# An adaptive feed-forward layer with a router in float32: the last four groups' first layer in two pairs by Strassen's algorithm

## The chip, the cores and the metric

The kernel runs on one core of one Trainium2 chip. Its time is the device time of one execution in microseconds, the median over several runs. Engines: PE is TensorE (matmuls), PEld its weight loads, DVE is VectorE, ACT is ScalarE, POOL is GpSimd, SP is the queue that issues most DMAs.

## What is computed

The reference, cut to its core (64 batches of N = 64 rows of D = 512; E = 6 experts of rank R = 16, the best 2 of them by router; biases and reshapes kept where they matter):

```
q_emb = relu(cond @ W3 + b3)                       # (64, 512)
x1 = (64 * x + sum(x, axis=1)) * q_emb[:, None, :] # (64, 64, 512)
y  = relu(x1 @ W2 + b2)                            # first layer, 512 x 512
gates = softmax(y @ W_router + b_router)           # 6 experts
w = gates where among the two largest, else 0
out = x + (y @ W_base + b_base) + (y @ A_s) @ B_s \
        + sum over e of w_e * ((y @ A_r[e]) @ B_r[e])
```

## The kernel before

The 4096 rows are cut into 8 groups of 512 (TG). In a group everything is transposed: features stand on the 128 partitions, in 4 chunks (KC, index c or k), rows along the free dimension. float32 accuracy comes from splitting each operand into two rounded parts, hi = round(a) and lo = a - hi (the *rest*), both of type float32r, and from three matmuls for each product: hi.hi, hi.lo, lo.hi (helper `product`, line 750).

Per group, by engine:

- **VectorE** makes the next group's x1 chunk by chunk: `turn_x` (line 474) transposes, `sum_x` (479) sums over the rows of a batch, `add_sum` (486) adds 64 x and the sum. It also makes the rests of x1 and of y (`x1_rest` 494, `y_rest` 500), the ranking of experts and the gates (`rank_experts` 547 to 570, `gates` 576 to 594), the weighted hidden layer (`weigh` 601, `hw_rest` 614) and the last addition of x (`add_x` 628).
- **GpSimd** multiplies by q_emb (`scale`, 308) and, at the start, makes the rests of the weights (`W_rest`, 314).
- **ScalarE** rounds: `x1_split` (347), `relu` (353 and 355, two instructions for each of the 4 output blocks m), `hw_split` (415); it copies the router's logits out of PSUM (`h_head`, 445, four instructions) and takes exponentials (454).
- **TensorE** runs 48 matmuls of the first layer (`m1`, four output blocks m of 12), 12 of `h` (router, shared and routed down projections in one), 48 of `m2` (y @ W_base, by 4 row tiles t), 12 of `up` (the up projections, onto the same PSUM banks as `m2`): 120 of 512 columns. `up` of group g-1 stands between the third and fourth block of m1 of group g.
- **SP** loads x twice (transposed quarters for VectorE, and as it is for the last addition), spreads the gates over the 16 ranks by four DMAs from `wT` to `gatesT`, and stores the output.

Each engine works through its own list in the order in which it is written; the engines meet in semaphores only. In the last group the gates are spread by one matmul (`expand`, 877) and hw is done in two halves. The 8 banks of PSUM are four of m2, three of m1 (the fourth block of m1 shares a bank with m2) and one, hT, for h.

## Time and profile before

| what | value |
|---|---|
| median of three runs | 235.28 us (235.24 to 235.88) |
| the profiled execution | 236.26 us, its span 234.1 us |
| TensorE busy | 229.5 us (98% of the span), 1007 matmuls |
| VectorE, ScalarE, GpSimd busy | 165.8, 86.4, 48.9 us |
| mean granted clock of TensorE | 1.000 |

The span runs from the first instruction to the last. The rows below are from this one execution; times in them are microseconds from the span's start, unless marked ns. "x3" behind a row is the number of instructions merged in it, and a bracket tells how long the engine had been idle before, and for whom. Matmuls overlap, so the 389 ns of one are not the step from one to the next.

### The profile page before, as it was taken

To read this page: it belongs to the slowest core of one execution; us is meant where nothing else is said; L and a number is where in the kernel's file an instruction comes from. 1 tells how busy PE (TensorE), PEld (TensorE's weight loads), DVE (VectorE), ACT (ScalarE), POOL (GpSimd) and SP (SyncE) were. 2 spreads that over 40 slices of the span, in tenths; PEclk is the share of its full clock that TensorE was granted. 3 is DMA by queue.
4 is the path that set the end of the run, shared out by engine and by line. 5 is a ranking of instruction groups with operands and counts; after the bars stand their busy time and mean duration, and the time that the engine had idled before them with its cause. 6 is when DMAs were issued, how large, how long until landed. Compare 5 with 4: busy or idle time off the path is not lost.

```text
span 234.1 us, 3090 instructions
## 1 busy us (share of the span) xinstructions
PE 229.5 (98%) x1007; PEld 188.3 (80%) x1007; DVE 165.8 (71%) x309; ACT 86.4 (37%) x171; POOL 48.9 (21%) x57
## 2 busy tenths in 40 slices
PE   7999999999999999999999999999999999999994
PEld 3977888888888888888888888888888888888883
DVE  0685979899889966596939969399656966064344
ACT  3178632646036330535116240263306351252430
POOL 6089334032212211013012211022111030000000
PEclk9999999999999999999999999999999999999999
DMA  6999903509270723626053641709020360104004
GB/s 207 313 229 229 276 5 79 137 3 315 67 187 4 250 111 69 144 107 255 10 134 69 194 167 26 185 4 345 12 34 0 141 218 14 21 0 179 3 0 179
DMA packets 32505, 28.80 MB, mean 123 GB/s; under 512 B 5817, under 2 KB 22909, under 8 KB 32494
## 3 DMA queue, kind: packets, MB, share of 16 engines
q1 hardware_dynamic: 30682, 28.50, 43.1%
q10 hardware_dynamic: 1812, 0.17, 0.6%
q8 instruction: 6, 0.10, 0.2%
q14 instruction: 5, 0.04, 0.0%
HBM read 18.89 MB, written 8.39 MB: 117 GB/s over the span
## 4 chain that ended last, share of the span: by engine, by line
PE 97%; DVE 1%; ACT 1%; issue 0%; DVEq 0%
PE m_ps L750 78%; PE hT L750 9%; PE m_ps L777 5%; PE m_ps L727 2%; DVE out_nat L628 1%; PE m_ps L740 1%; PE m_ps L769 1%; PE hT L740 0%; ACT qT L367 0%; ACT W_hi L373 0%; ACT x_hi L378 0%; PE m_ps L734 0%; DVE idle L468 0%; PE hT L877 0%; PE m_ps L733 0%
## 5 line engine op out<-in xcount | busy, mean ns | idle before, releaser
L308 POOL TENSOR_TENSOR x_full<-x_sum,qT 128x512 f32<-128x512 f32 x28 | 32.2, 1150 | 134.6 <-DVE x_sum L486 134.6
L353 ACT ACTIVATE y_hi<-m_ps,condT 128x512 fp32r<-128x512 f32 x32 | 22.0, 687 | 77.5 <-PE m_ps L750 77.2
L750 PE MATMUL m_ps<-Wb_lo,y_hi 128*128 128x512 f32 x128 | 49.8, 389 | 0.0
L750 PE MATMUL m_ps<-Wb_hi,y_lo 128*128 128x512 f32 x128 | 49.8, 389 | 0.0
L750 PE MATMUL m_ps<-Wb_hi,y_hi 128*128 128x512 f32 x128 | 49.8, 389 | 0.0
L750 PE MATMUL m_ps<-x_hi,W_hi 128*128 128x512 f32 x112 | 43.6, 389 | 0.0
L750 PE MATMUL m_ps<-x_hi,W_lo 128*128 128x512 f32 x112 | 43.6, 389 | 0.0
L500 DVE TENSOR_TENSOR y_lo<-m_ps,y_hi 128x512 fp32r<-128x512 f32 x32 | 21.6, 674 | 30.4 <-ACT m_ps L355 30.4
L750 PE MATMUL m_ps<-x_lo,W_hi 128*128 128x512 f32 x112 | 41.8, 389 | 0.0
L474 DVE STREAM_TRANSPOSE xT<-x_quart 128x512 f32<-128x512 f32 x28 | 30.3, 1083 | 0.0
L750 PEld LDWEIGHTS m_ps<-Wb_hi,y_hi 128*128 128x128 f32 x128 | 24.0, 188 | 5.0
L750 PEld LDWEIGHTS m_ps<-Wb_hi,y_lo 128*128 128x128 f32 x128 | 24.0, 188 | 5.0
L750 PEld LDWEIGHTS m_ps<-Wb_lo,y_hi 128*128 128x128 f32 x128 | 24.0, 188 | 5.0
L347 ACT ACTIVATE x_hi<-x_full 128x512 fp32r<-128x512 f32 x28 | 17.6, 629 | 19.1 <-POOL x_full L308 19.0
L750 PEld LDWEIGHTS m_ps<-x_hi,W_hi 128*128 128x128 f32 x112 | 21.0, 188 | 4.4
L750 PEld LDWEIGHTS m_ps<-x_hi,W_lo 128*128 128x128 f32 x112 | 21.0, 188 | 4.4
L750 PEld LDWEIGHTS m_ps<-x_lo,W_hi 128*128 128x128 f32 x112 | 21.0, 188 | 4.3
L628 DVE TENSOR_TENSOR out_nat<-m_ps,x_nat 128x512 f32<-128x512 f32 x32 | 20.5, 680 | 2.1 <-PE m_ps L750 2.1
L355 ACT ACTIVATE m_ps<-m_ps,condT 128x512 f32<-128x512 f32 x32 | 21.0, 655 | 0.0
L486 DVE SCALAR_TENSOR_TENSOR x_sum<-xT,vsum 128x512 f32<-128x512 f32 x28 | 19.4, 693 | 2.1
L494 DVE TENSOR_TENSOR x_lo<-x_full,x_hi 128x512 fp32r<-128x512 f32 x28 | 19.1, 706 | 1.6 <-ACT x_hi L347 1.6
L479 DVE TENSOR_REDUCE vsum<-xT 128x8 f32<-128x512 f32 x28 | 19.0, 679 | 0.3
(99 smaller groups left out, 256.5 us busy)
## 6 DMA issues: line engine op xcount, KB each, us to landing
out_dram<-out_nat SPq DMA_DIRECT2D x32, 256.0 KB, 2.2
x_quart<-in_x_dram SPq DMA_DIRECT2D x28, 256.0 KB, 4.5
x_nat<-in_x_dram SPq DMA_DIRECT2D x7, 1024.0 KB, 6.1
gatesT<-wT SPq DMA_DIRECT2D x28, 48.0 KB
x_nat<-in_x_dram SPq DMA_DIRECT2D x4, 256.0 KB, 3.7
W_f<-in_L_cond_W_dram SPq DMA_DIRECT2D x4, 256.0 KB, 6.7
Wb_f<-in_L_ffn_W_base_dram SPq DMA_DIRECT2D x1, 1024.0 KB, 9.2
W_sb<-in_L_cond_W_dram SPq DMA_DIRECT2D x2, 256.0 KB, 5.0
```

What stands on the lines that cost most here:

```text
L308: nc.gpsimd.tensor_tensor(per_batch(x1_full[:, c, :]), per_batch(x1_sum[:, c, :]), qT[:, c, bass.ds(BG * g, BG)].unsqueeze(2).to_broadcast ...
L347: nc.scalar.activation(x1_hi[par][:, c, :], x1_full[:, c, :], ACT.Copy).then_inc(x1_hi_ready, 1)
L353: nc.scalar.activation(y_hi[:, m, :], m1_ps[m][:, :], ACT.Relu, bias=b2_sb[:, m:m + 1]).then_inc(y_hi_ready, 1)
L355: nc.scalar.activation(m1_ps[m][:, :], m1_ps[m][:, :], ACT.Relu, bias=b2_sb[:, m:m + 1]).then_inc(y_full_ready, 1)
L474: nc.vector.transpose(xT[c % 2][:, :], x_quart[par][:, :, :].rearrange("p b (i c) -> p c b i", c=KC)[:, c]).then_inc(xT_ready, 1)
L479: nc.vector.tensor_reduce(vsum[c % 2][:, :], per_batch(xT[c % 2][:, :]), AX.X, ALU.add).then_inc(vsum_ready, 1)
L486: nc.vector.scalar_tensor_tensor(out=per_batch(x1_sum[:, c, :]), in0=per_batch(xT[c % 2][:, :]), scalar=float(N), in1=vsum[c % 2][:, :].un ...
L494: nc.vector.tensor_tensor(x1_lo[par][:, c, :], x1_full[:, c, :], x1_hi[par][:, c, :].bitcast(F32), ALU.subtract).then_inc(x1_lo_ready, 1)
L500: nc.vector.tensor_tensor(y_lo[:, m, :], m1_ps[m][:, :], y_hi[:, m, :].bitcast(F32), ALU.subtract).then_inc(y_lo_ready, 1)
L628: nc.vector.tensor_tensor(out_nat[par][:, t, :], m2_ps[t][:, :], x_nat[par][:, t, :], ALU.add).then_inc(out_ready, 1)
L750: mm = nc.tensor.matmul(psum, lhsT, rhs, start=start and i == 0, stop=stop and i == len(terms) - 1)
L777: return nc.tensor.matmul(m1_ps[m][:, :], W[:, k, m * P:(m + 1) * P], x1[0][:, k, :], start=k == 0 and W is W2_hi and x1 is x1_hi, stop=k ...
```

## The change

Groups 4 to 7 are done as pairs p = 0 (groups 4, 5) and p = 1 (groups 6, 7). The first layer of a pair is a product of 2 x 2 blocks: W2 cut into halves of output features m and of input features k, x1 into halves of k and the two groups. It is done by Winograd's form of Strassen's algorithm with seven block products instead of eight. With x11, x21 the two halves of k of the first group and x12, x22 those of the second:

- operands: T1 = x12 - x11, T2 = x22 - T1, T3 = x22 - x12, T4 = x21 - T2, each in two chunks kk = 0, 1; and weights V1 to V4, combined once from W2's quarters;
- products 1 to 7 (`PRODUCTS`), each of 6 matmuls for each half-block mh of m; TensorE runs them in `PRODUCT_ORDER`;
- results: C11, C12, C21, C22 by seven additions for each mh (`ADD_ORDER`), in VectorE, in place in PSUM, with ScalarE's copy of product 1 (`copy_p1`).

GpSimd combines the operands and makes all their rests (`prepare`), and the rests of group 3's x1 too. ScalarE rounds the 14 operands (`operand`). The chunks of a pair come in the order of `CHUNKS` as (group of the pair, c). Tiles are shared to make room: x1 is worked on in place (`xs`), hw in place in hT, the output in place in `x_nat`, so that loads of x wait for stores. The four loops over groups are written out. The `expand` matmul and the work in halves of the last group go; its gates are spread by DMA into `gates_last`.

The core of the diff (blank lines left out). The orders:

```diff
+        CHUNKS = ((0, 0), (1, 0), (1, 2), (0, 2), (0, 1), (0, 3), (1, 1), (1, 3))
+        OPERANDS = (("x11", 0), ("T1", 0), ("x22", 0), ("T2", 0), ("T3", 0), ("x21", 0), ("T4", 0),
+                    ("x11", 1), ("x21", 1), ("T1", 1), ("T2", 1), ("T3", 1), ("x22", 1), ("T4", 1))
+        COMBOS = (("T1", 0), ("T2", 0), ("T3", 0), ("T4", 0), ("T1", 1), ("T2", 1), ("T3", 1), ("T4", 1))
+        SLOTS = {("x11", 0): 8, ("T1", 0): 9, ("T2", 0): 10, ("x22", 0): 11, ("T3", 0): 12, ("x21", 0): 13, ("T4", 0): 0,
+                 ("x11", 1): 1, ("x21", 1): 2, ("T1", 1): 3, ("T2", 1): 4, ("T3", 1): 5, ("x22", 1): 6, ("T4", 1): 7}
+        PRODUCTS = {1: ("W", 0, 0, "x11", 0), 2: ("W", 2, 0, "x21", 1), 3: ("V", 2, 0, "x22", 2), 4: ("W", 2, 256, "T4", 3),
+                    5: ("V", 2, 256, "T1", 3), 6: ("V", 0, 0, "T2", 2), 7: ("V", 0, 256, "T3", 0)}
+        PRODUCT_ORDER = ((1, 2, 6, 7, 3, 5, 4), (1, 2, 6, 5, 7, 4, 3))
+        USED_BY = {operand: n for n, (_, _, _, operand, _) in PRODUCTS.items()}
+        ADD_ORDER = (("C11", "u2", "u4", "u3", "C22", "C12", "C21"), ("C11", "u2", "u4", "u3", "C22", "C21", "C12"))
+        C_BANK = {"C11": 1, "C22": 0, "C12": 2, "C21": 3}
+        Y_ORDER = ((0, 0), (1, 2), (1, 0), (0, 2), (0, 1), (1, 3), (0, 3), (1, 1))
```

GpSimd, one pair (`rest` waits for `operand` of ScalarE; `scale_pair` for VectorE's chunk):

```diff
+                scale_pair(0, 0)
+                rest("x11", 0)
+                scale_pair(1, 0)
+                T1(0)
+                scale_pair(1, 2)
+                rest("T1", 0)
+                rest("x22", 0)
+                T2(0)
+                T3(0)
+                rest("T2", 0)
+                scale_pair(0, 2)
+                rest("T3", 0)
+                rest("x21", 0)
+                T4(0)
+                scale_pair(0, 1)
+                rest("T4", 0)
+                rest("x11", 1)
+                scale_pair(0, 3)
+                scale_pair(1, 1)
+                rest("x21", 1)
+                T1(1)
+                scale_pair(1, 3)
+                rest("T1", 1)
+                T2(1)
+                T3(1)
+                rest("T2", 1)
+                rest("T3", 1)
+                rest("x22", 1)
+                T4(1)
+                rest("T4", 1)
+            for p in range(PAIRS):
+                prepare(p)
```

ScalarE, from group 3 on:

```diff
+            def operand(p, name, kk):
+                if name[0] == "T":
+                    act.wait_ge(combo_ready, nth_combo(p, name, kk))
+                else:
+                    act.wait_ge(pair_full_ready, nth_chunk(p, {"x11": 0, "x21": 0, "x22": 1}[name], kk + (0 if name == "x11" else 2)))
+                if p > 0:
+                    act.wait_ge(product_done, nth_product(p - 1, 1, USED_BY[name]))
...
+                x1_split(3, m - 1)
+            head(2)
+            exponentials(2)
+            x1_split(3, 3)
+            operand(0, "x11", 0)
+            relu(3, 0)
+            operand(0, "T1", 0)
+            hw_split(2)
+            relu(3, 1)
+            operand(0, "x22", 0)
+            operand(0, "T2", 0)
+            relu(3, 2)
+            operand(0, "T3", 0)
+            operand(0, "x21", 0)
+            relu(3, 3)
+            operand(0, "T4", 0)
+            operand(0, "x11", 1)
+            head(3)
+            exponentials(3)
+            operand(0, "x21", 1)
+            operand(0, "T1", 1)
+            def pair(p):
...
+                copy_p1(0)
+                operand(p, "T2", 1)
+                hw_split(g - 1)
+                operand(p, "T3", 1)
+                operand(p, "x22", 1)
+                relu_pair(0, 0)
+                operand(p, "T4", 1)
+                relu_pair(1, 2)
+                copy_p1(1)
+                relu_pair(1, 0)
+                relu_pair(0, 2)
+                operand_next("x11", 0)
+                relu_pair(0, 1)
+                relu_pair(1, 3)
+                relu_pair(0, 3)
+                relu_pair(1, 1)
+                operand_next("T1", 0)
+                head(g)
+                operand_next("x22", 0)
+                operand_next("T2", 0)
+                exponentials(g)
+                head(g + 1)
+                operand_next("T3", 0)
+                operand_next("x21", 0)
+                exponentials(g + 1)
+                operand_next("T4", 0)
+                operand_next("x11", 1)
+                hw_split(g)
+                operand_next("x21", 1)
+                operand_next("T1", 1)
+            for p in range(PAIRS):
+                pair(p)
+            hw_split(NG - 1)
```

VectorE, from the end of group 2 on (`whole_pair` is turn, sum and add of one chunk; `..._next` the same for the next pair):

```diff
+            rank_experts(2)
+            gates(2)
+            whole_pair(0, 0)
+            whole_pair(0, 1)
+            whole_pair(0, 2)
+            y_rest_single(3, 0)
+            weigh(2)
+            turn_pair(0, 3)
+            hw_rest(2)
+            y_rest_single(3, 1)
+            total_pair(0, 3)
+            add_x(2, 0)
+            y_rest_single(3, 2)
+            add_x(2, 1, 2, 3)
+            whole_pair(0, 4)
+            y_rest_single(3, 3)
+            whole_pair(0, 5)
+            rank_experts(3)
+            gates(3)
+            whole_pair(0, 6)
+            whole_pair(0, 7)
...
+                weigh(g - 1)
+                C11(0)
+                u_2(0)
+                hw_rest(g - 1)
+                turn_next(0)
+                y_rest_pair(0, 0)
+                sum_next(0)
+                add_x(g - 1, 0, 1)
+                u_4(0)
+                u_3(0)
+                C22(0)
+                C12(0)
+                C21(0)
+                add_x(g - 1, 2, 3)
+                y_rest_pair(1, 2)
+                C11(1)
+                y_rest_pair(1, 0)
+                u_2(1)
+                add_next(0)
+                u_4(1)
+                y_rest_pair(0, 2)
+                u_3(1)
+                C22(1)
+                C21(1)
+                y_rest_pair(0, 1)
+                C12(1)
+                y_rest_pair(1, 3)
+                y_rest_pair(0, 3)
+                y_rest_pair(1, 1)
+                turn_next(1)
+                total_next(1)
+                turn_next(2)
+                total_next(2)
                 rank_experts(g)
+                turn_next(3)
+                gates(g)
+                total_next(3)
+                rank_experts(g + 1)
+                turn_next(4)
+                gates(g + 1)
+                total_next(4)
+                weigh(g)
+                turn_next(5)
+                hw_rest(g)
+                total_next(5)
+                turn_next(6)
+                total_next(6)
+                if not more:
+                    weigh(g + 1)
+                add_x(g, 0, 1, 2, 3)
+                turn_next(7)
+                total_next(7)
+            for p in range(PAIRS):
+                pair(p)
```

TensorE, one pair:

```diff
+                    which, k0, col, operand, b = PRODUCTS[n]
+                    W_hi, W_lo = (W2_hi, W2_lo) if which == "W" else (V_hi, V_lo)
+                    cols = slice(col + mh * P, col + (mh + 1) * P)
+                    ps = m1_pair[p][mh][b][:, :]
+                    for kk in range(2):
+                        begins = kk == 0
+                        if mh == 0:
+                            pe.wait_ge(pair_hi_ready, nth_operand(p, operand, kk))
+                        product(ps, [(W_hi[:, k0 + kk, cols], hi_of(operand, kk)),
+                                     (W_lo[:, k0 + kk, cols], hi_of(operand, kk))], begins, False)
+                        if mh == 0:
+                            pe.wait_ge(pair_lo_ready, nth_operand(p, operand, kk))
+                        mm = product(ps, [(W_hi[:, k0 + kk, cols], lo_of(operand, kk))], False, kk == 1)
+                    mm.then_inc(product_done, 1)
+                if p > 0:
+                    pe.wait_ge(out_ready, TT * (g - 2) + TT)
+                blocks(0, 1)
+                blocks(0, 2)
+                if p == 0:
+                    pe.wait_ge(V_lo_ready, KC)
+                blocks(0, 6)
+                pe.wait_ge(p1_copied, 2 * p + 1)
+                blocks(0, 7)
+                pe.wait_ge(adds_ready, nth_add(p, 0, "u2"))
+                blocks(0, 3)
+                up(g - 1, 0, 1)
+                blocks(0, 5)
+                up(g - 1, 2, 3)
+                pe.wait_ge(adds_ready, nth_add(p, 0, "u4"))
+                blocks(0, 4)
+                pe.wait_ge(out_ready, TT * (g - 1) + 1)
+                blocks(1, 1)
+                pe.wait_ge(out_ready, TT * (g - 1) + 2)
+                blocks(1, 2)
+                pe.wait_ge(out_ready, TT * (g - 1) + 3)
+                blocks(1, 6)
+                pe.wait_ge(out_ready, TT * (g - 1) + 4)
+                blocks(1, 5)
+                pe.wait_ge(p1_copied, 2 * p + 2)
+                blocks(1, 7)
+                pe.wait_ge(adds_ready, nth_add(p, 1, "u4"))
+                blocks(1, 4)
+                blocks(1, 3)
+                h(g, 0)
+                h(g, 2)
+                m2(g, 0, 0, 2)
+                h(g, 1)
+                m2(g, 0, 1)
+                h(g, 3)
+                m2(g, 0, 3)
+                for k in range(KC):
+                    h(g + 1, k)
+                for t in range(1, TT):
+                    m2(g, t, *range(KC))
+                m2(g + 1, 0, *range(KC))
+                m2(g + 1, 1, *range(KC))
+                up(g, 0, 1, 2, 3)
+                m2(g + 1, 2, *range(KC))
+                pe.wait_ge(out_ready, TT * g + 1)
+                m2(g + 1, 3, *range(KC))
+                if last:
+                    up(g + 1, 0, 1, 2, 3)
```

## Rows read from the trace of the kernel before

**Rows 1.** The page: busy time by engine, and the chain's shares by engine.

```profile
PE 229.5 (98%) x1007; PEld 188.3 (80%) x1007; DVE 165.8 (71%) x309; ACT 86.4 (37%) x171; POOL 48.9 (21%) x57
...
PE 97%; DVE 1%; ACT 1%; issue 0%; DVEq 0%
```

**Rows 2.** The chain that ended last: start us, length us, what.

```profile
1.27 3.59 PE m_ps L727 x8
...
12.47 11.47 PE m_ps L777 x48
...
82.44 23.12 PE m_ps L750 x102
...
109.64 23.12 PE m_ps L750 x102
...
225.92 0.23 PE hT L877
```

**Rows 3.** Timeline of VectorE: start us, length us, line, operation, count.

```profile
60.36 1.07 DVE L474 STREAM_TRANSPOSE xT<-x_quart 128x512 f32<-128x512 f32 x1
...
62.80 0.68 DVE L494 TENSOR_TENSOR x_lo<-x_full,x_hi 128x512 fp32r<-128x512 f32 x1
...
87.00 1.25 DVE L494 TENSOR_TENSOR x_lo<-x_full,x_hi 128x512 fp32r<-128x512 f32 x2
...
90.71 1.09 DVE L474 STREAM_TRANSPOSE xT<-x_quart 128x512 f32<-128x512 f32 x1
...
95.99 0.69 DVE L500 TENSOR_TENSOR y_lo<-m_ps,y_hi 128x512 fp32r<-128x512 f32 x1 [4.19 <-ACT m_ps L355]
...
102.05 1.87 DVE L628 TENSOR_TENSOR out_nat<-m_ps,x_nat 128x512 f32<-128x512 f32 x3
...
111.22 0.31 DVE L547 STREAM_TRANSPOSE h_nat<-h_head 128x128 f32<-128x128 f32 x1 [1.79 <-ACT h_head L445]
...
113.24 0.17 DVE L576 TENSOR_REDUCE den<-expo 128x4 f32<-128x24 f32 x1
...
114.20 1.25 DVE L494 TENSOR_TENSOR x_lo<-x_full,x_hi 128x512 fp32r<-128x512 f32 x2
```

**Rows 4.** Who waited for whom: us in total, times, longest us.

```profile
POOL x_full L308 <- DVE x_sum L486: 134.6, 28, 7.6
```

**Rows 5.** Timeline of GpSimd: two rests, and one scale.

```profile
13.75 2.54 POOL L314 TENSOR_TENSOR W_lo<-W_f,W_hi 128x512 fp32r<-128x512 f32 x2 [0.67 <-ACT W_hi L373]
...
36.30 1.04 POOL L308 TENSOR_TENSOR x_full<-x_sum,qT 128x512 f32<-128x512 f32 x1 [4.85 <-DVE x_sum L486]
```

**Rows 6.** Timeline of ScalarE in group 3.

```profile
98.48 0.65 ACT L355 ACTIVATE m_ps<-m_ps,condT 128x512 f32<-128x512 f32 x1
99.05 0.63 ACT L347 ACTIVATE x_hi<-x_full 128x512 fp32r<-128x512 f32 x1
100.16 0.69 ACT L353 ACTIVATE y_hi<-m_ps,condT 128x512 fp32r<-128x512 f32 x1 [0.48 <-PE m_ps L750]
...
109.68 1.50 ACT L445 ACTIVATE h_head<-hT,h_bias 32x128 f32<-32x128 f32 x4 [1.58 <-PE hT L750]
```

**Rows 7.** Timelines of VectorE and GpSimd where the two meet.

```profile
30.84 0.66 DVE L551 TENSOR_TENSOR logit<-h_nat,lmax 128x24 f32<-128x24 f32 x1
...
30.16 1.29 POOL L314 TENSOR_TENSOR Wu_lo<-Wu_f,Wu_hi 128x512 fp32r<-128x512 f32 x1
...
125.87 0.69 DVE L614 TENSOR_TENSOR hw_lo<-hw_full,hw_hi 128x512 fp32r<-128x512 f32 x1
...
126.21 1.25 POOL L308 TENSOR_TENSOR x_full<-x_sum,qT 128x512 f32<-128x512 f32 x1 [6.90 <-DVE x_sum L486]
```

**Rows 8.** The instructions of line 551: shortest, median, longest ns.

```profile
L551 DVE TENSOR_TENSOR logit<-h_nat,lmax x8: 182/182/657, 30.8 to 220.6; 128x24 f32<-128x24 f32 x8
```

**Rows 9.** Timeline of SP's queue: issues.

```profile
114.31 3.75 SPq L263 DMA_DIRECT2D gatesT<-wT  x4
```

**Rows 10.** Windows: busy us of each engine, then the granted clock.

```profile
91.90:119.10 27.20, 27.20 (x122) 22.53 (x121) 20.46 (x38) 9.38 (x18) 4.58 (x5) 1.00 0.43 124
```

More of the change, by code:

```diff
@@ L265, in _ @@
-            step(0, 0, first=True)
-            with sp.Fori(0, (NG - 4) // 2) as pair:
-                for half in range(2):
-                    step(pair * 2 + (1 + half), (1 + half) % 2)
-            for g in range(NG - 3, NG):
-                step(g, g % 2)
-            store(NG - 1, (NG - 1) % 2, (1, 2, 3, 4))
+                    sp.wait_ge(out_ready, TT * g + 1 + max(order.index(i) for i in range(t + 1)))
+                    sp.dma_start(out_groups[g][:, t, :], x_nat[g % 2][:, t, :]).then_inc(stored[g % 2], 16)
@@ new lines, in _ @@
+            for m in range(KC):
+                relu(0, m)
+            act.wait_ge(Wu_loaded, 48)
+            nc.scalar.activation(Wu_hi[:, :], Wu_f[:, :], ACT.Copy).then_inc(Wu_hi_ready, 1)
+            x1_split(1, 0)
+            head(0)
+            x1_split(1, 1)
+            exponentials(0)
+            x1_split(1, 2)
+            x1_split(1, 3)
+            hw_split(0)
+            for m in range(KC):
+                relu(1, m)
+                if m >= 2:
+                    x1_split(2, m - 2)
@@ new lines, in _ @@
+            head(1)
+            x1_split(2, 2)
+            exponentials(1)
+            act.wait_ge(V_step, 4)
+            act.wait_ge(Wb_lo_ready, KC)
+            for c in range(KC):
+                V_round(c)
+            x1_split(2, 3)
+            relu(2, 0)
+            hw_split(1)
+            for m in range(1, KC):
+                relu(2, m)
+                x1_split(3, m - 1)
[3 more added lines that the diff above has]
+            operand(0, "x11", 0)
@@ new lines, in _ @@
+            total(1, 2)
+            turn_x(1, 3)
+            total(1, 3)
+            for c in range(KC):
+                x1_rest(1, c)
+            weigh(0)
+            hw_rest(0)
+            turn_x(2, 0)
+            total(2, 0)
+            add_x(0, 0)
+            y_rest_single(1, 0)
+            turn_x(2, 1)
+            y_rest_single(1, 1)
+            total(2, 1)
+            y_rest_single(1, 2)
+            add_x(0, 1, 2, 3)
+            turn_x(2, 2)
+            y_rest_single(1, 3)
@@ new lines, in _ @@
+            total(2, 2)
+            x1_rest(2, 0)
+            rank_experts(1)
+            gates(1)
+            x1_rest(2, 1)
+            turn_x(2, 3)
+            total(2, 3)
+            x1_rest(2, 2)
+            x1_rest(2, 3)
+            turn_x(3, 0)
+            total(3, 0)
+            turn_x(3, 1)
+            y_rest_single(2, 0)
+            weigh(1)
+            total(3, 1)
+            hw_rest(1)
+            y_rest_single(2, 1)
+            turn_x(3, 2)
+            add_x(1, 0)
@@ L722, in _ @@
+            for p in range(PAIRS):
+                pair(p)
+            hw_rest(NG - 1)
+            add_x(NG - 1, 0, 1, 2, 3)
         @block.tensor
@@ L933 @@
+            for g in range(PAIRED):
+                single(g)
+            for p in range(PAIRS):
+                pair(p)
 _INS = ['x', 'cond_1024', 'L0_cond_W3', 'L0_cond_b3', 'L0_cond_W2', 'L0_cond_b2', 'L0_ffn_W_base', 'L0_ffn_b_base',
```

792 lines of the change are left out of this document (426 added, 366 removed).

## The prediction

> **What bounds the kernel now.** Read the page's busy shares first, then the chain that ended last: TensorE is busy for 98% of the span and makes up 97% of the chain [rows 1, 2]. The pieces of the chain show how: from 12.47 us on there is no wait in it, and a matmul of 512 columns starts every 23.12 / 102 = 0.2267 us [rows 2]. (The 389 ns in the groups is the length of one; neighbours overlap.) So one group, 120 matmuls, is 27.2 us, and one matmul less is worth 0.2267 us as long as TensorE never waits. Then read each of the other engines in order of time: how much slack is there inside a group? In group 3 VectorE works from 87.00 to 91.8, waits 4.2 us for a relu, and is then busy to 114 but for the 1.8 us before the gates [rows 3]; it has some 6 us to spare in 27.2. ScalarE has more. GpSimd waits 134.6 us in all [rows 4]. The first matmul of group 4 starts at 109.64 + 42 x 0.2267 - 0.16 = 119.0 (the chain counts by ends, 0.16 later).
>
> **What is taken away.** Per pair, 2 x 48 matmuls become 2 x 7 x 6 = 84: 24 fewer in two pairs, 24 x 0.2267 = 5.44 us. The expand matmul goes too, 0.23 [rows 2]. Together **-5.67 us**. The tail after the last up product (four adds and a store) stays.
>
> **What is added, by engine, per pair.** GpSimd: 8 scales of 1.04, and 8 combinations and 14 rests, which read two full tiles as W_rest does, 1.27 each [rows 5]: 8.3 + 27.9 = 36.3 us in a pair of 51.7. VectorE: 14 adds that recombine the products, at 0.6 each [rows 3] 8.5 us, less 8 rests (4.8) that GpSimd takes over. ScalarE: 14 roundings and 2 copies in place of 8 roundings, 8 x 0.57 = 4.6 us. None of these is over its budget, so totals decide nothing. What decides is order: product 6, third on TensorE, needs T2 of both k, and T2(1) needs chunk 7, the last chunk that VectorE makes.
>
> **Wait 1, the start of the first pair.** Follow VectorE from the end of the gates of group 2, at 87.0. A chunk (turn, sum, add) is 2.44 us [rows 3]. Chunks 0 to 2 end at 94.3. y_rest(3,0) and weigh keep their times; chunk 3 ends at 101.1. Now ScalarE: rounding T2(0) stands ahead of relu(3,2). On GpSimd T2(0) comes after rest T1 and rest x22, whose rounding itself waits behind relu(3,1): it ends at 102.25. So relu(3,2), which ran at 100.16 before [rows 6], ends at 104.05, y_rest(3,2) and three adds of x end at 106.5, chunk 4 at 108.95, y_rest(3,3) at 109.55 (0.3 us late for TensorE), chunk 5 at 112.0. ScalarE must round T4(0) and x11(1) before head(3), so head runs 111.35 to 112.85 instead of 109.68 to 111.18 [rows 6]. Ranking and gates take 3.0 [rows 3]: 115.9. Only then come chunks 6 and 7, to 120.8. GpSimd, which had nothing to do from 114.3 to 118.3, then has scale, rest T1, T2, T3, rest T2: 1.04 + 4 x 1.27 = 6.1 us, and 1.2 us of backlog: 128.1. TensorE wants that tile for the 18th matmul of the pair, at 119.0 + 17 x 0.2267 = 122.85. **5.25 us.** The floor: if every earlier wait were hidden, head would still end at 111.2, gates at 114.2, chunk 7 at 119.1, and GpSimd with scale(1,1), rest x21, T1 in between at 126.3: 3.45 us. The wait can't go below that as the orders are written.
>
> **Wait 2, up(4) in the middle of the first pair.** VectorE's last y_rest of the pair ends 3.0 us after h(4,0) starts (C12 is added 0.8 after the last product, then a relu of 1.2 on ScalarE behind one that is still running, then 0.6). From there to weigh(4) its list adds up to 16.5 us (four chunks 9.8, two rankings 4.0, two gates 2.0, weigh 0.7), hw takes 0.6 on ScalarE, and up(4) starts 96 matmuls = 21.8 us after h(4,0): 1.7 us to spare if VectorE never idles. But head(4) stands behind the rounding of T1(0), which needs chunk 1, GpSimd's scale and T1: 2.0 us of idle on VectorE; the exponentials of 4 stand behind T2(0): 0.8 more; hw_split(4) stands behind x11(1), which needs chunk 4 and its scale: 1.0. That is 3.8, less 1.7 to spare 2.1, and hw_rest ends 0.25 after the third matmul of up wants it: **2.35 us** (floor 0).
>
> **Wait 3, the start of the second pair.** Chunks 5 and 6, four adds of x and chunk 7 follow hw_rest(4) on VectorE: 1.35 + 2.44 + 2.4 + 2.44 = 8.6 us, and GpSimd's 6.1 behind it: 14.7. TensorE gets from there to product 6 in 34 + 17 matmuls = 11.6: **3.05 us** (with VectorE never idle since the last y_rest, 1.4).
>
> **Meetings of VectorE and GpSimd.** The logit subtraction of 24 elements takes 182 ns, but 657 ns in group 0, where it ended when GpSimd's Wu_rest ended; a scale takes 1.04, but 1.25 where it began beside hw_rest [rows 7, 8]. Both of VectorE's operands lie in SBUF there. In before the two engines hardly meet, since GpSimd is idle; now it has back-to-back work while VectorE adds chunks, ranks and gates. A meeting costs VectorE 0.475 by the row; nothing is the lower bound, a whole rest of 1.27 the upper. I take the row. Four meetings lie on the path of wait 1 (add of chunk 4, logit, diff, add of chunk 7): +1.9. Nine on wait 2 (an add, and logit, diff, tie, beats of both groups): 4.3, less the 0.8 of idle that they fill: +3.5. One on wait 3: +0.45. The Trainium skill has the rule, in "SBUF — State Buffer", section "Who interferes with whom": a VectorE instruction with two SBUF inputs and a GpSimd instruction that reads SBUF exclude each other for the whole instruction. The trace agrees in the one meeting shown; by the rule a meeting could cost up to a whole rest, as in the third rival.
>
> **What costs nothing, and under what.** V's four combinations and rests (8 x 1.27 = 10.2 us) lie in GpSimd's idle of groups 1 and 2 and are wanted 50 us later; uncovered they would be 10.2 us. The gates of the last group go through SP instead of a matmul: its four DMAs take 3.75 us to issue [rows 9] and stand behind those of group 6, but h(7) now ends 96 matmuls, 21.8 us, before up(7); head, gates, two such issues and weigh are some 15. Loads of x into the tiles that were stored from wait for those stores and still come most of a group early. Products of the second half of m wait for adds that end about 0.5 us before they are wanted; that is the thinnest cover, and if it went each of some 4 adds would cost 0.6.
>
> **The sum.** Waits 5.25 + 2.35 + 3.05 = 10.65, meetings 1.9 + 3.5 + 0.45 = 5.85: 16.5. Less 5.67: **+10.8 us**. The profiled execution took 236.26 (span 234.1), 0.98 over the median of the three runs, 235.28. 236.26 + 10.8 = 247.1, by the median 246.1: forecast **246**.
>
> **The rivals.** *Meetings cost nothing*: only the waits of order stay, +5.0, 240.3. For it: in before only one logit in eight was slow. Against: there was hardly anything to meet. *The other side, VectorE runs ahead*: if ScalarE's roundings never hold up relu, head and hw_split, VectorE never idles, and waits are 3.45 + 0 + 1.4 = 4.85, less 5.67: -0.8, 234.5. It decides from the point where the three waits together are under 5.7. Against it: for that, T2(0) must be rounded before 100.2, where GpSimd can't have it before 102. *Full price*: each meeting costs a GpSimd instruction; step by step the waits become 9.2, 9.6 and 4.0, +17.1, 252.4. *The clock falls in the waits*: the granted clock is 1.00, 2.4 GHz, in every stretch of before [rows 10], so no row has the lower level. The nearest row is the start, where the first eight matmuls after idleness took 3.59 / 8 = 0.449 each, twice the pitch [rows 2]. Eight such after each of two long waits are 2 x 8 x 0.222 = +3.6, 249.7. (The Trainium skill, "TensorE: Matmul & The Clock Gate", section "Part 1", has the clock halved after TensorE idles; no row here shows it.) *The change doesn't do what it says*, that is, the matmuls don't get fewer: the loops over PRODUCTS count 84, so I give it nothing.
>
> **How the numbers follow.** Forecast 0.42; meetings free 0.24; full price or clock or both 0.18; VectorE ahead 0.16. Under 0.3% (0.7 us) a measurement of this kernel can't tell a change from none. The last case straddles that: 0.10 faster, 0.06 same. The rest is slower: 0.84. The range reaches from the upper part of the last case, 235, to above full price, 254; what is left out is 0.10 below and some 0.07 above. Within the slower cases alone it is 239 to 254.
>
> **What would show it.** TensorE's chain has three breaks: in product 6 of the first pair, released by ScalarE's T2 and then by GpSimd's rest of T2; before up(4), released by ScalarE's hw; and in product 6 of the second pair. Chunk 7's turn starts after the gates of group 3, near 118 to 122. Logit, diff and the adds of chunks take longer in the pairs than they do in before. Matmuls number 982. I am wrong if up and product 6 follow without a break, if logit stays at 182 ns, or if TensorE waits elsewhere, above all in the second half of m or for the last gates.

## The result, and the profile after

The change makes the kernel slower: 252.53 us (252.08 to 255.3) against 235.35, a ratio of 1.075 with an interval of 1.067 to 1.083. The forecast was slower, 246, with a range of 235 to 254. So the sign and the range held, and the likeliest value was 6.5 short.

The profiled execution took 252.3 us, its span 249.8, which is 15.7 over the span before. The page of the kernel after answers to [rows 1]: busy time, the granted clock in 40 slices in tenths, and the chain's shares.

```profile
PE 230.2 (92%) x982; PEld 185.9 (74%) x982; DVE 186.8 (75%) x313; ACT 93.6 (37%) x181; POOL 118.8 (48%) x107
...
PEclk9999999999999999999976999999569999999999
...
PE 39%; DVE 36%; POOL 14%; ACT 6%; issue 4%; DVEq 0%; POOLq 0%; ACTq 0%
```

The matmuls did get fewer, 1007 to 982 (the 24 and the expand). But TensorE's share of the chain falls from 97% to 39%, and VectorE's rises from 1% to 36%: the kernel is now bound by the preparation of operands. The granted clock has two dips, and they tell where to look. The timeline of TensorE after (start us, length us; the bracket is the wait and who ended it), at its breaks in group 3, in product 6 of the first pair, before up(4), and in product 6 of the second pair:

```profile
111.02 0.50 PE L1179 MATMUL hT<-y_lo,Wd_hi 128*128 128x512 f32 x1 [1.76 <-DVE y_lo L785]
...
124.08 0.39 PE L1179 MATMUL m_ps<-x_lo_more,V_hi 128*128 128x512 f32 x1
128.69 0.79 PE L1179 MATMUL m_ps<-x_hi,V_hi 128*128 128x512 f32 x1 [4.22 <-ACT x_hi L640]
129.28 0.63 PE L1179 MATMUL m_ps<-x_hi,V_lo 128*128 128x512 f32 x1
130.48 0.79 PE L1179 MATMUL m_ps<-x_lo,V_hi 128*128 128x512 f32 x1 [0.57 <-POOL x_lo L474]
131.07 0.63 PE L1179 MATMUL m_ps<-x_hi_more,V_hi 128*128 128x512 f32 x1
...
134.91 0.40 PE L1179 MATMUL m_ps<-x_hi,V_hi 128*128 128x512 f32 x1
...
172.15 0.39 PE L1179 MATMUL m_ps<-Wb_hi,y_lo 128*128 128x512 f32 x1
180.27 0.79 PE L1179 MATMUL m_ps<-Wu_hi,hw_hi 128*128 128x512 f32 x1 [7.74 <-ACT hw_hi L610]
180.86 0.63 PE L1179 MATMUL m_ps<-Wu_lo,hw_hi 128*128 128x512 f32 x1
...
185.98 0.46 PE L1179 MATMUL m_ps<-Wb_lo,y_hi 128*128 128x512 f32 x1
...
195.75 0.50 PE L1179 MATMUL m_ps<-x_lo,V_hi 128*128 128x512 f32 x1 [0.47 <-POOL x_lo L474]
```

The window behind the second long break (busy us of PE, PEld, DVE, ACT, POOL, then the granted clock):

```profile
180.00:185.00 5.00, 4.73 (x11) 3.72 (x12) 4.65 (x7) 0.85 (x2) 2.77 (x4) 0.50 0.21 43
```

Read a break as the step between two starts less the usual step of 0.2267 (the pitch). In product 6 of the first pair it is 4.38 and 0.97, before up(4) 7.89, in product 6 of the second pair 0.62, and in group 3, where h waits for y_rest(3,3), 1.92. With 0.42 for hw_lo of group 1 (at 72.89, in group 2) that makes 16.2. Then look at the rows behind the two long breaks: a matmul starts every 0.427 until 134.91 and until 185.98, with a granted clock of 0.50 in the window (0.51 from 130 to 135). Over the pitch these stretches cost 0.36 + 0.36 + 9 x 0.2 = 2.5 and 0.36 + 12 x 0.2 = 2.8, together 5.3. The account then closes: from the first matmul of the first layer (11.66, before 12.47) to the last of the kernel (246.21, before 230.52) the time grew from 218.05 to 234.55, by 16.5, and 16.5 + 5.67 = 22.2, of which breaks and slow stretches are 16.2 + 5.3 = 21.5. The forecast had named three breaks; that in group 3 is a fourth, and that in group 2 a fifth.

Why are the operands late? The timeline of VectorE after, in the first pair, answers to [rows 7]: an add of a chunk alone and one beside GpSimd, then the rankings of groups 4 and 5, weigh and hw_rest:

```profile
155.53 0.69 DVE L928 SCALAR_TENSOR_TENSOR xs<-xs,vsum_pair 128x512 f32<-128x512 f32 x1
...
157.99 1.28 DVE L928 SCALAR_TENSOR_TENSOR xs<-xs,vsum_pair 128x512 f32<-128x512 f32 x1
160.82 0.31 DVE L831 STREAM_TRANSPOSE h_nat<-h_head 128x128 f32<-128x128 f32 x1 [1.55 <-ACT h_head L620]
...
161.71 1.34 DVE L839 TENSOR_TENSOR diff<-logit 128x144 f32<-128x144 f32 x1
163.09 1.29 DVE L845 SCALAR_TENSOR_TENSOR tie<-diff,earlier 128x144 f32<-128x144 f32 x1
164.41 1.28 DVE L850 SCALAR_TENSOR_TENSOR tie<-diff,tie 128x144 f32<-128x144 f32 x1
...
169.74 0.69 DVE L835 TENSOR_TENSOR logit<-h_nat,lmax 128x24 f32<-128x24 f32 x1
170.47 1.34 DVE L839 TENSOR_TENSOR diff<-logit 128x144 f32<-128x144 f32 x1
171.84 1.27 DVE L845 SCALAR_TENSOR_TENSOR tie<-diff,earlier 128x144 f32<-128x144 f32 x1
173.15 1.25 DVE L850 SCALAR_TENSOR_TENSOR tie<-diff,tie 128x144 f32<-128x144 f32 x1
...
177.86 0.75 DVE L876 SCALAR_TENSOR_TENSOR m_ps<-m_ps,h_bias,gatesT 128x512 f32<-128x512 f32 x1
...
180.25 0.69 DVE L882 TENSOR_TENSOR hw_lo<-m_ps,hw_hi 128x512 fp32r<-128x512 f32 x1 [0.63 <-ACT hw_hi L610]
```

And GpSimd at the same time:

```profile
160.35 2.54 POOL L474 TENSOR_TENSOR x_lo_more<-xs,x_hi_more 128x512 fp32r<-128x512 f32 x2
162.84 1.37 POOL L487 TENSOR_TENSOR xs<-xs 128x512 f32<-128x512 f32 x1
164.16 1.36 POOL L493 TENSOR_TENSOR xs<-xs 128x512 f32<-128x512 f32 x1
165.48 1.36 POOL L474 TENSOR_TENSOR x_lo_more<-xs,x_hi_more 128x512 fp32r<-128x512 f32 x1
...
179.03 2.51 POOL L474 TENSOR_TENSOR x_lo<-xs,x_hi 128x512 fp32r<-128x512 f32 x2
```

Put the ends side by side. diff, tie and the second tie end at 163.05, 164.38 and 165.69, each just after one of GpSimd's instructions. An instruction that takes 0.31 takes 1.3 here: it waits until GpSimd's whole instruction is over, and then GpSimd's next one waits for it (1.37 instead of 1.27). hw_lo at 180.25 has one operand in PSUM and takes its usual 0.69 while two rests run. VectorE's busy time, 165.8 in [rows 1], is now 186.8; how much of that is waiting, e3 tells below. Two lines after (shortest/median/longest ns), of which the first answers to [rows 8], show that not every instruction pays: the logit of 182 ns is lengthened in five groups of eight, to between 0.30 and 0.69, and diff in two, but there to four times its length:

```profile
L835 DVE TENSOR_TENSOR logit<-h_nat,lmax x8: 183/388/695, 30.0 to 224.3; 128x24 f32<-128x24 f32 x8
L839 DVE TENSOR_TENSOR diff<-logit x8: 307/310/1340, 30.7 to 224.5; 128x144 f32<-128x144 f32 x8
```

### The profile page after: what moved, and what is told of

Read it like the earlier page. It is cut to its first block, busy times and chain, and to the rows that moved or that the text cites. A ratio compares the mean times of both kernels' runs of the same rounds, so it can differ in the third digit from the quotient of the medians.

```text
span 249.8 us, 2832 instructions
## 1 busy us (share of the span) xinstructions
PE 230.2 (92%) x982; PEld 185.9 (74%) x982; DVE 186.8 (75%) x313; ACT 93.6 (37%) x181; POOL 118.8 (48%) x107
## 4 chain that ended last, share of the span: by engine, by line
PE 39%; DVE 36%; POOL 14%; ACT 6%; issue 4%; DVEq 0%; POOLq 0%; ACTq 0%
PE m_ps L1179 25%; PE hT L1179 6%; POOL xs L398 5%; PE m_ps L1209 5%; DVE xs L914 3%; DVE xs L928 3%; DVE xs L758 3%; POOL x_lo L474 3%; DVE x_nat L894 3%; DVE vsum_pair L921 2%; POOL xs L480 2%; DVE xs L770 2%; DVE x_lo L779 2%; DVE vsum L764 2%; DVE y_lo L785 2%
## 5 line engine op out<-in xcount | busy, mean ns | idle before, releaser
L398 POOL TENSOR_TENSOR xs<-xs,qT 128x512 f32<-128x512 f32 x28 | 30.4, 1087 | 66.2 <-DVE xs L928 36.7
L1179 PEld LDWEIGHTS m_ps<-Wb_hi,y_lo 128*128 128x128 f32 x116 | 21.8, 188 | 4.6
L894 DVE TENSOR_TENSOR x_nat<-m_ps,x_nat 128x512 f32<-128x512 f32 x29 | 18.8, 685 | 8.3 <-PE m_ps L1179 8.2
L1179 PE MATMUL m_ps<-x_hi,W_hi 128*128 128x512 f32 x61 | 23.8, 390 | 0.0
L1179 PE MATMUL m_ps<-x_hi,W_lo 128*128 128x512 f32 x61 | 23.7, 389 | 0.0
L1179 PE MATMUL m_ps<-x_lo,W_hi 128*128 128x512 f32 x61 | 22.0, 389 | 0.0
L474 POOL TENSOR_TENSOR x_lo<-xs,x_hi 128x512 fp32r<-128x512 f32 x16 | 20.4, 1289 | 1.5 <-ACT x_hi L640 1.5
L1179 PE MATMUL m_ps<-Wu_hi,hw_hi 128*128 128x512 f32 x29 | 12.2, 420 | 7.7 <-ACT hw_hi L610 7.7
L914 DVE STREAM_TRANSPOSE xs<-x_quart 128x512 f32<-128x512 f32 x16 | 17.4, 1085 | 0.0
L474 POOL TENSOR_TENSOR x_lo_more<-xs,x_hi_more 128x512 fp32r<-128x512 f32 x12 | 16.0, 1342 | 2.6 <-ACT x_hi_more L640 2.6
L928 DVE SCALAR_TENSOR_TENSOR xs<-xs,vsum_pair 128x512 f32<-128x512 f32 x16 | 15.0, 934 | 0.5
```

The lines of the kernel that those rows point to most:

```text
L398: return nc.gpsimd.tensor_tensor(per_batch(tile), per_batch(tile), qT[:, c, BG * g:BG * (g + 1)].unsqueeze(2).to_broadcast([P, BG, N]), AL ...
L474: nc.gpsimd.tensor_tensor(lo_of(name, kk), tile_of(name, kk), hi_of(name, kk).bitcast(F32), ALU.subtract).then_inc(pair_lo_ready, 1)
L894: nc.vector.tensor_tensor(x_nat[g % 2][:, t, :], m2_of[g][t][:, :], x_nat[g % 2][:, t, :], ALU.add).then_inc(out_ready, 1)
L914: nc.vector.transpose(xs[half][:, c, :], x_quart[half][:, :, :].rearrange("p b (i c) -> p c b i", c=KC)[:, c]).then_inc(pair_turned, 1)
L928: nc.vector.scalar_tensor_tensor(out=per_batch(xs[half][:, c, :]), in0=per_batch(xs[half][:, c, :]), scalar=float(N), in1=vsum_pair[i % 2] ...
L1179: mm = nc.tensor.matmul(psum, lhsT, rhs, start=start and i == 0, stop=stop and i == len(terms) - 1)
```

## The experiments

The theory: meetings of the two engines at the price of a whole GpSimd instruction, the waits of the written orders, and the lower clock after the two long breaks make up the loss. Rivals: the orders alone do it; the clock is a mere symptom; or VectorE is simply over its budget. e1, e2 and e7 change the kernel before, the others the kernel after.

**e1 and e2, reading beside writing.** In the kernel before, GpSimd gets extra work behind the scales of each of groups 2 to 7: four additions of two SBUF tiles, or nine memsets that last about as long.

```diff
+            def extra(i):
+                nc.gpsimd.tensor_tensor(W2_f[:, i % 2, :], W2_f[:, 2, :], W2_f[:, 3, :], ALU.add).then_inc(extra_done, 1)
...
+                for i in range(4):
+                    pool.wait_ge(extra_done, 4 * (g - 2) + i + 1)
+                    extra(i)
```

(in e2: `memset(W2_f[:, i % 2, :], 1.0)`, nine times)

> The kernel before, with four additions of two full SBUF tiles on GpSimd after the last scale of each group from group 2 on, beside the gates; their results are used by nobody. If a VectorE instruction with both inputs in SBUF and a GpSimd instruction that reads SBUF exclude each other for the whole instruction, logit, diff, tie and beats take about 1.2 to 1.3 us each in groups 2 to 6, while the sums over free elements (lmax, rank, den) keep their 0.17 to 0.30; the time stays within 1 us of before, since VectorE has the slack. If a meeting costs only the 0.475 that the one row of before shows, they take 0.66 to 0.8. If the two don't disturb each other, 0.18 and 0.31.

> The same with nine fills of a tile on GpSimd, some 0.52 us each, which write and read nothing. If only reading SBUF excludes, logit, diff, tie and beats stay at 0.18 and 0.31. If any work of GpSimd on SBUF does, each takes some 0.3 to 0.5 more.

e1 took 238.71 and e2 235.84, one run each, beside 235.79 for the kernel before on the same chip. The same instructions of the ranking in e1 and then in e2 (shortest/median/longest ns), and e2's GpSimd in one group:

```profile
L564 DVE TENSOR_TENSOR diff<-logit x8: 307/308/309, 32.5 to 223.5; 128x144 f32<-128x144 f32 x8
...
L570 DVE SCALAR_TENSOR_TENSOR tie<-diff,earlier x8: 307/1282/1287, 32.8 to 223.8; 128x144 f32<-128x144 f32 x8
...
L575 DVE SCALAR_TENSOR_TENSOR beats<-diff,tie x8: 307/1330/1335, 33.2 to 224.2; 128x144 f32<-128x144 f32 x8
```

```profile
L570 DVE SCALAR_TENSOR_TENSOR tie<-diff,earlier x8: 307/308/308, 31.5 to 220.8; 128x144 f32<-128x144 f32 x8
```

```profile
110.13 5.19 POOL L333 MEMSET W_f<- 128x512 f32 x9
```

With a GpSimd that reads, tie and beats cost 1.0 more each, in the five groups 2 to 6; with one that is as busy writing, nothing. Logit took 0.82 to 0.93 in these groups, less than was expected. GpSimd's own four additions took 5.55 in all, 1.39 each. That a small instruction slips in undelayed (diff, 308 in all eight, right behind a delayed logit) shows that not every VectorE instruction that could meet one pays. So the engines do not meet in semaphores only, as the description of the kernel before has it. The time of e1 rose by 2.9, where less than 1 was expected. Its only breaks in TensorE over 0.4 are 0.73 at the start, for a DMA, and 0.71 at 56.60, for y_lo; its first layer began at 13.41 instead of 12.47. A single run with such a start can't price a meeting in time; it shows the duration alone. The Trainium skill, "SBUF — State Buffer", section "Who interferes with whom", has the rule: a VectorE instruction with two SBUF inputs contends with a GpSimd instruction that reads SBUF, not with one that only writes it. These two runs agree, 1282 against 308 ns.

**e3, no meetings.** In the kernel after, each combination and rest of the pairs becomes two memsets of the same tile. This leaves out the T operands and the low parts of the pairs' x1; semaphores, orders and matmuls stay. The scales, and the rests of V's tiles, still read SBUF.

```diff
-                    nc.gpsimd.tensor_tensor(lo_of(name, kk), tile_of(name, kk), hi_of(name, kk).bitcast(F32),
-                                            ALU.subtract).then_inc(pair_lo_ready, 1)
+                    write_only(lo_of(name, kk).bitcast(F32)).then_inc(pair_lo_ready, 1)
...
+            def write_only(tile):
+                nc.gpsimd.memset(tile, 0.0).then_inc(written, 1)
+                pool.wait_ge(written, count[0] + 1)
+                count[0] += 1
+                return nc.gpsimd.memset(tile, 0.0)
```

> The kernel after, with each combination and each rest of the pairs on GpSimd replaced by two fills of the same tile with zeros (1.04 us in place of 1.27), so the operands T and all low parts of the pairs are left out; order, waits and the rest of the work stay. If meetings of VectorE and GpSimd make most of the waits beyond those of the written order, diff, tie and beats go back to 0.31, the wait before up of group 4 falls from 7.9 to under 3.5, and the time is 239 to 244. If the written order alone makes the waits, and the meetings only fill idle time, 249 or more.

It took 242.95 us (240.21 to 243.32), ratio 1.027 (1.020 to 1.033): 9.6 less than the changed kernel. In the profiled executions the stretch from the first matmul of the first layer to the last of the kernel is 11.5 shorter (234.55 - 223.05); e9 tells why the two differ. From its page, and then from TensorE's timeline:

```profile
PE 228.6 (95%) x982; PEld 185.1 (77%) x982; DVE 176.8 (73%) x313; ACT 93.5 (39%) x181; POOL 105.8 (44%) x151
```

```profile
125.24 0.50 PE L1184 MATMUL m_ps<-x_hi,V_hi 128*128 128x512 f32 x1 [1.95 <-ACT x_hi L645]
...
170.23 0.50 PE L1184 MATMUL m_ps<-Wu_hi,hw_hi 128*128 128x512 f32 x1 [2.15 <-ACT hw_hi L615]
```

The same 313 instructions of VectorE are busy for 176.8 instead of 186.8: ten microseconds of meetings. Some stay: logit still takes 0.70 at 162.62, beside a scale, but diff and both ties are back at 0.31. The break in group 3 is gone; that before up(4) is 2.30. Not all of the 9.6 is meetings, since two memsets step by some 1.05 us where a rest steps by 1.25. Four of them stand in a row ahead of product 6, so about 0.8 there is the memsets' speed.

**e4, TensorE kept busy.** In the kernel after, 18 more matmuls in product 6 of the first pair and 32 before up(4) add other products to sums that are open.

```diff
+            def keep_warm_in(ps, n):
+                for _ in range(n):
+                    nc.tensor.matmul(ps, Wb_hi[:, 0, 0:P], Wb_hi[:, 0, :], start=False, stop=False)
...
+                        if mh == 0 and n == 6 and kk == 1 and p == 0:
+                            keep_warm_in(ps, 18)
...
+                if not last:
+                    keep_warm_in(m2_of[g + 1][1][:, :], 32)
                 up(g, 0, 1, 2, 3)
```

> The kernel after with 18 matmuls put into the first wait (product 6 of the first pair) and 32 into the second (before up of group 4), which add other products to the open sums, so that TensorE is busy while it waits. If the fall of the clock costs what its matmuls show after the waits (1.7 and 2.5 us), the granted clock stays at 1.00 and the first 1.7 is gained; the second is mostly eaten by the wait of the second pair's product 6, which hangs on VectorE and GpSimd: 249.5 to 251. If the clock is without effect on the end, since the other engines set it, 252.5.

It took 250.33 us (250.08 to 251.11), ratio 1.062 (1.060 to 1.065): 2.2 less, with more matmuls. From its page, and then from TensorE's timeline in product 6 of the second pair:

```profile
PEclk9999999999999999999999999999999999999999
```

```profile
192.49 0.50 PE L1179 MATMUL m_ps<-x_hi,V_hi 128*128 128x512 f32 x1 [1.47 <-ACT x_hi L640]
...
194.28 0.50 PE L1179 MATMUL m_ps<-x_lo,V_hi 128*128 128x512 f32 x1 [1.06 <-POOL x_lo L474]
```

The granted clock is 0.999 for the whole execution, so all 5.3 us of slow stretches are gone, but only 2.2 come back. The second pair's product 6 now waits 1.63 + 1.22 = 2.85 by the steps, where it waited 0.62: the slow matmuls behind up(4) had been giving VectorE and GpSimd time.

**e9, both.** e3 with ten such matmuls at each of the two places.

```diff
+                            keep_warm_in(ps, 10)
...
+                    keep_warm_in(m2_of[g + 1][1][:, :], 10)
```

> The run without meetings, with 10 more matmuls in product 6 of the first pair and 10 more ahead of up(4), which add other products to sums that are open. They fill 2.27 us each of waits of 2.1 and 2.3. Theory (what is left of the loss besides meetings and waits is the lower clock level after the waits, in proportion about half of the 2.2 us that it cost in the changed kernel): granted clock at least 0.995, time 241.3 to 242.3. Rival (waits that short cost no clock, the 0.982 is only idle time): 242.8 to 243.6, since the fillers stand a little beyond the waits.

It took 239.22 us, the median of four executions (three from 239.04 to 239.34, and one of 329.46, at a mean granted clock of 0.66, that nothing here explains), ratio 1.0145 (1.0115 to 1.0175). In the profiled execution the granted clock is 1.0. That is below what was expected, and 3.7 less than e3, but the traces show that the clock makes less than half of the 3.7. From the first matmul of the first layer to the last of the kernel, e3 takes 223.05 us (12.32 to 235.38) and e9 221.61 (12.09 to 233.70): 1.4 less. Another 2.1 lie behind the last matmul of e3, which is this one, in a span of 241.1:

```profile
235.38 0.39 PE L1184 MATMUL hT<-Wu_hi,hw_lo 128*128 128x512 f32 x1
```

From its start to the end of the span are 5.7 us, and 3.6 in every other trace of this case. VectorE's last addition ends 1.1 us after that start in e3 as in e9, so the last stores took longer; why is open, and e3's other executions left no trace. The clock was thus worth 1.4, near the 1.1 that was expected, though e3's slow stretches are 1.5 and 1.8 by the steps of its matmuls: in e9 the second pair's product 6 waits 1.27 + 0.88, where it waited 0.80 in e3, as between the changed kernel and e4. The step from e4 to e9, both at full clock and both with 3.6 behind the last matmul, is 250.33 - 239.22 = 11.1 us, the meetings with what the memsets save.

**e5, chunks 6 and 7 ahead of the ranking of group 3.** A test of the order behind the first long break.

```diff
             whole_pair(0, 5)
-            rank_experts(3)
-            gates(3)
             whole_pair(0, 6)
             whole_pair(0, 7)
+            rank_experts(3)
+            gates(3)
```

(and on ScalarE `exponentials(3)` behind `operand(0, "T1", 1)`)

> The kernel after with VectorE's chunks 6 and 7 of the first pair ahead of the ranking and gates of group 3 (and ScalarE's rounding of x21 and T1 ahead of the exponentials). If VectorE has too much to do in this stretch, the wait moves: product 6 waits some 2 us less, but the gates of group 3 come about 8 us later and up of group 3 waits 5 us or more for hw: 254 to 259. If it is only that chunk 7 stands behind the gates, the wait at product 6 shrinks and nothing takes its place: 246 to 249.

It took 258.31 us in one run, within the first range, but the break stands elsewhere than was said. Product 6 waits only 1.12 + 1.28 now, but the next product stops TensorE:

```profile
137.51 0.80 PE L1179 MATMUL m_ps<-x_hi,V_hi 128*128 128x512 f32 x1 [8.58 <-ACT x_hi L640]
```

ScalarE's rounding of T3(1) stands behind hw_split(3), which waits for the later gates. The break moved and grew.

**e6, the gates of the pair's first group early**, on VectorE right behind chunk 1 and on ScalarE with head, exponentials and hw ahead of the roundings.

```diff
                 turn_next(1)
                 total_next(1)
+                rank_experts(g)
+                gates(g)
                 turn_next(2)
                 total_next(2)
-                rank_experts(g)
                 turn_next(3)
-                gates(g)
                 total_next(3)
+                turn_next(4)
+                weigh(g)
+                total_next(4)
+                hw_rest(g)
                 rank_experts(g + 1)
-                turn_next(4)
+                turn_next(5)
                 gates(g + 1)
-                total_next(4)
-                weigh(g)
-                turn_next(5)
-                hw_rest(g)
                 total_next(5)
```

> The kernel after with the ranking and gates of a pair's first group right behind VectorE's chunk 1 of the next pair, those of its second group behind hw_rest, and ScalarE's heads, exponentials and hw ahead of the roundings that hold them up. If VectorE is over its budget in the pair, up of group 4 no longer waits, but the second pair's product 6 waits 5 us or more: 247 to 251. If ScalarE's order is the cause, both waits go: 242 to 245.

It took 257.0 us (256.77 to 257.11), ratio 1.089 (1.087 to 1.092): outside what either theory said. up(4) waits 1.55 in place of 7.89, and then the last m2 of the first pair waits for the adds of x of group 4:

```profile
187.71 0.79 PE L1179 MATMUL m_ps<-Wb_hi,y_hi 128*128 128x512 f32 x1 [6.97 <-DVE x_nat L894]
```

I took that for a VectorE over its budget because of the meetings. e8 tests it.

**e8, e6's order and e3's memsets together**, the two diffs above in one kernel (T operands and low parts left out as in e3).

> The written order of the run with the gates first, together with the write-only GpSimd work of the run without meetings (T operands and low parts of the pairs left out). Theory (the meetings put VectorE over its budget in a pair, and a new order can only move the wait to what VectorE does last): without meetings VectorE has time to spare, so the 7.1 us that TensorE waited for the adds of x of group 4 fall under 2.5, and the time is 239 to 243.5, no worse than the 242.95 without meetings alone. Rival (that order is bad in itself, since add_x of group 4 stands behind both gates and five chunks): the wait for the adds of x stays over 4 us and the time is 244.5 to 250.

It took 248.52 us (248.16 to 249.65), ratio 1.053 (1.051 to 1.056): the rival's numbers, and 5.6 worse than e3 (8.4 from the first matmul to the last, since e3 lost 2.1 behind it). The wait for the adds of x falls only to 4.43. The timeline of VectorE in e8 shows why:

```profile
164.43 0.76 DVE L881 SCALAR_TENSOR_TENSOR m_ps<-m_ps,h_bias,gatesT 128x512 f32<-128x512 f32 x1 [1.33 <-DMA gatesT<-wT]
...
168.59 0.69 DVE L887 TENSOR_TENSOR hw_lo<-m_ps,hw_hi 128x512 fp32r<-128x512 f32 x1 [2.08 <-ACT hw_hi L615]
169.97 0.31 DVE L836 STREAM_TRANSPOSE h_nat<-h_head 128x128 f32<-128x128 f32 x1 [0.69 <-ACT h_head L625]
```

VectorE idles 4.1 us there, once for the spread of the gates and twice for a ScalarE that is itself behind a rounding. So in e6 the order costs 4.4 of the 7.1 and the meetings 2.7. In the second pair the same m2 stops both runs once more, by 2.95 in e6 and 2.96 in e8, again for an addition of x (TensorE and then VectorE in e8):

```profile
237.09 0.50 PE L1184 MATMUL hT<-Wb_hi,y_hi 128*128 128x512 f32 x1 [2.80 <-DVE x_nat L899]
```

```profile
235.69 0.76 DVE L881 SCALAR_TENSOR_TENSOR m_ps<-m_ps,h_bias,x_quart 128x512 f32<-128x512 f32 x1 [6.11 <-DMA x_quart<-Wu_f]
```

The adds of x of group 6 stand behind weigh of group 7, and in this order its gates come late. That break is as long with the meetings as without. My budget theory fell: that order has its own waits.

**e7, 24 matmuls fewer and nothing else.** The kernel before without six low-order products of the first layer in each of groups 3 to 6.

```diff
+                    if not isinstance(g, int) and (m == 1 or m == 2 and k < 2):
+                        terms = terms[:2]
```

> The kernel before with 24 matmuls of the first layer left out (six low-order products in each of groups 3 to 6), and nothing else changed: what the matmuls saved would be worth alone. If TensorE alone bounds the kernel, 24 x 0.2267 = 5.4 us less, 229.9. If VectorE or the gates are close behind, less than half of it, over 232.5.

It took 232.57 us (232.21 to 232.93), ratio 0.9855 (0.984 to 0.987): 3.2 less, not 5.4: over the 232.5 of the second expectation, but more than the half of 5.4 that went with it. In each of the four groups a break of 0.35 appears at the third matmul of up, as here:

```profile
125.89 0.50 PE L750 MATMUL m_ps<-Wu_hi,hw_lo 128*128 128x512 f32 x1 [0.19 <-DVE hw_lo L614]
```

These are 1.4 of the 2.2 that are missing, and 1.9 with the matmul behind each, which starts another 0.11 late. hw_lo has little slack in the order of the kernel before, so there 24 matmuls taken out free of charge are worth some 3 us. For the order of the pairs e7 shows nothing.

## Why the forecast was right in sign and short in size

**The saving, -5.67: right** as a term; the account above closes with it. In the order of the kernel before it would have been worth less (e7).

**Wait 1: right as a sum, 7.15 forecast with its meetings, 7.27 measured,** as 1.92 in group 3 and 5.35 in product 6. That the sum is right is luck, for its two terms err in opposite ways. Without the pairs' meetings (e9) the wait is 2.27 of added matmuls and 0.83, together 3.1, or 3.9 with the 0.8 that the memsets save; the forecast had 5.25 for the order. That leaves 3.4 for the meetings, where 1.9 were forecast: the adds of chunks 4, 5 and 7 and logit lengthened by 1.03, 1.1, 0.5 and 0.5. And y_rest(3,3), which I had 0.3 late, stood behind the first of these; the timeline of VectorE after, in order:

```profile
108.64 1.72 DVE L928 SCALAR_TENSOR_TENSOR xs<-xs,vsum_pair 128x512 f32<-128x512 f32 x1
110.29 0.68 DVE L785 TENSOR_TENSOR y_lo<-m_ps,y_hi 128x512 fp32r<-128x512 f32 x1
...
117.96 1.05 DVE L914 STREAM_TRANSPOSE xs<-x_quart 128x512 f32<-128x512 f32 x1
```

That break also made TensorE later for product 6. Chunk 6's turn starts at 117.96, 2.1 after the 115.9 of the forecast.

**Wait 2: the mechanism right, the price of a meeting wrong.** 5.85 forecast, 7.89 measured. By the forecast's own steps: TensorE gives 21.8 us; VectorE's last y_rest ends 3.1 after h starts (3.0 forecast); from there to weigh are 24.2, which is the list of 15.8, meetings of 7.1 and idleness of 1.3 (4.3 and 2.8 forecast); hw_hi waits 1.1 behind x11(1) (1.0 forecast). With 0.7 for weigh and 0.6 for hw_hi that is 29.7, 7.9 more than TensorE gives. Without the pairs' meetings the wait is 2.31 (e3), as forecast for the order (2.35). ScalarE after:

```profile
179.10 0.63 ACT L640 ACTIVATE x_hi<-xs 128x512 fp32r<-128x512 f32 x1 [4.21 <-POOL xs L398]
179.64 0.58 ACT L610 ACTIVATE hw_hi<-m_ps 128x512 fp32r<-128x512 f32 x1
```

The step that failed is "A meeting costs VectorE 0.475 by the row". Of the nine meetings counted on this path, the six of diff and the ties cost 0.98 each and the other three 0.6, 0.5 and 0.1. I took the one row there was, with the upper bound beside it: the slow logit of [rows 7] had begun when half of GpSimd's rest was over, and against back-to-back work the wait is up to a whole instruction (diff, 1.03 of 1.27). The trace of before held a dearer meeting, which neither [rows 3] nor [rows 8] show: one of the 28 x1_rests (line 494) took 1.53 us in place of 0.68, beside a scale.

**Wait 3: 3.5 forecast, 0.62 measured,** and not since the step was wrong: VectorE and GpSimd took 14.8 us from hw_rest to the rest of T2, as forecast (14.7). TensorE took 2.2 longer to get there, at the lower clock; with that taken away the wait is 2.85 (e4).

**The clock: held as a rival, missing in the sum.** The granted clock falls to 0.50, that is 1.2 of 2.4 GHz, after the two long breaks, 5.3 us of slow stretches, and is worth 2.2 us in the end (e4), where the rival had 3.6. The Trainium skill, "TensorE: Matmul & The Clock Gate", section "Part 1", says that idleness halves the clock; here the trace agrees, with steps of 0.427 against 0.2267.

**The rival of the full price** gave 252.4, and 252.53 was measured. Its mechanism is the one that e3 shows, but its terms are not: it had breaks of 9.2, 9.6 and 4.0, and measured were 7.27, 7.89 and 0.62 with slow stretches in place of the rest. That its total fits so well is chance.

**Meetings free: 240.3 forecast; e9 measures 239.22** without the pairs' meetings and with the clock held. So the waits of the written orders were about right in sum: forecast 10.65 in all, and 239.22 - 235.93 + 5.67 = 9.0 measured, some of it shortened by the memsets. One by one the three waits are 3.1, 2.3 and 2.15 without the meetings, for 5.25, 2.35 and 3.05. The loss over the 5.67 saved is then 9.0 of order, 11.1 of meetings, of which the faster memsets are a part, and 2.2 of clock: 22.3 of the 22.9 that 252.53 is over 235.35 less 5.67.

What was forecast to cost nothing cost next to nothing: no break over 0.3 stands in the second half of m, for V's tiles or before the last up. But V's rests are not quite free: beside them a rest of x1 and an add of VectorE take 1.10 and 1.18 (at 64.62 and 67.50), 0.9 more than alone, and hw_lo of group 1 then comes 0.42 late, in e3 and e9 too. What stays open is whether some order of the lists beats the kernel before; the two tried here moved the break and made it longer.

## What to carry to other kernels

Where another engine takes over work "in its idle time", look not only at its budget but at what its operands share with its neighbour: GpSimd work that reads SBUF can make a VectorE instruction with two SBUF operands wait for up to a whole GpSimd instruction (here 0.31 became 1.3), so the smallest instructions suffer the largest factor, and they stood on the critical chain here. Where both engines work back to back, price such a meeting at the length of the other engine's instruction, and not by one meeting that began when the other was half done. And when a kernel at 98% of TensorE loses matmuls, check first what else ends within a microsecond of being needed: in e7 hw_lo alone took a third of the saving (1.9 of 5.4 us).

## What was not expected of the hardware

- The price depends on the length of the other's instruction, not on one's own: a ranking instruction went from 0.31 to 1.3 us, while GpSimd's went from 1.27 to 1.37 beside small instructions and to 1.74 at 122.78, beside an add that takes 0.69 alone.
- With one operand in PSUM no VectorE instruction was lengthened here: hw_lo took 0.69 beside two running rests, and none of the 32 y_rests of the kernel after took more than 0.69.
- A break of 1.92 us (at 111.02) left the granted clock at 1.00, while in e3 breaks of 2.11 and 0.86, with two matmuls between them, were followed by seven steps of 0.40 to 0.59. Time lost to a low clock is partly given back where another engine is late next: 2.2 of 5.3 us was all it cost in the changed kernel, and 1.4 of 3.4 in e3.
